# A second norm whose scale moves to the logits and gates, row sums taken from the attention values, one expert choice for all tokens, and a sum of experts on TensorE

## The reference

```python
def _L1_attn_ref(x):
    scores = jnp.einsum('bsd,btd->bst', x, x)
    attn_weights = jax.nn.softmax(scores, axis=-1)
    return jnp.einsum('bst,btd->bsd', attn_weights, x)

def _L1_ffn_ref(x, router_w, router_b, expert_w, expert_b):     # E = 8, K = 2
    router_probs = jax.nn.softmax(x @ router_w + router_b, axis=-1)
    top_p, top_i = jax.lax.top_k(router_probs, K)
    top_p = top_p / jnp.sum(top_p, axis=-1, keepdims=True)
    expert_out = jnp.einsum('bnd,edc->bnec', x, expert_w) + expert_b
    gathered = jnp.take_along_axis(expert_out, top_i[..., None], axis=2)
    return jnp.einsum('bnk,bnkc->bnc', top_p, gathered)

x = x + _L0_conv_ref(_gn(x), ...)
t = _to_tokens(x)
t = t + _L1_attn_ref(_ln_t(t))
t = t + _L1_ffn_ref(_ln_t(t), ...)
```

## Time and profile before

| | us |
|---|---|
| median of 3 executions | 107.4 (107.09 to 108.33) |
| profiled execution, its own time | 108.61 |
| its span | 106.9 |
| TensorE matmul busy (533 instructions) | 78.2 (73%) |
| VectorE busy (127) | 67.1 (63%) |
| GpSimd busy (73) | 44.1 (41%) |
| ScalarE busy (66) | 30.8 (29%) |
| mean granted TensorE clock | 0.837 |

### The profile page before, as it was taken

How to read it: one execution, slowest core, us unless ns; L and a number is a source line. 1 busy time by engine, 2 the same in 40 slices (tenths; PEclk the granted TensorE clock), 3 DMA queues, 4 the chain that set the end, 5 groups by cost and what they waited for, 6 DMA issues and landing times.

```text
span 106.9 us, 1448 instructions
## 1 busy us (share of the span) xinstructions
PE 78.2 (73%) x533; PEld 65.0 (61%) x533; DVE 67.1 (63%) x127; ACT 30.8 (29%) x66; POOL 44.1 (41%) x73
## 2 busy tenths in 40 slices
PE   3797999489801995599399965979448899957820
PEld 3696499389602994599399954956124588933400
DVE  2046200427968999907828934882997268989990
ACT  0441000696991410100740002154934130101100
POOL 6019999700526999999300000000003300494440
PEclk9999999999985599859999999999975555695555
DMA  0214300028400000000000000000000000000022
GB/s 26 83 32 92 62 8 0 6 65 257 123 0 3 0 0 0 0 0 6 3 0 0 0 0 3 6 0 0 0 0 0 0 6 0 0 0 0 3 46 53
DMA packets 5115, 2.36 MB, mean 22 GB/s; under 512 B 4290, under 2 KB 4643, under 8 KB 5107
## 3 DMA queue, kind: packets, MB, share of 16 engines
q1 hardware_dynamic: 4675, 2.06, 8.1%
q10 hardware_dynamic: 432, 0.20, 0.7%
HBM read 0.81 MB, written 0.26 MB: 10 GB/s over the span
## 4 chain that ended last, share of the span: by engine, by line
PE 40%; DVE 35%; ACT 11%; issue 6%; DMA 3%; DVEq 1%; POOL 1%; POOLq 0%
DVE image_all L936 8%; PE ps L580 7%; PE ps L492 7%; PE ps L532 5%; DVE prod L288 4%; DVE att_d L1084 4%; DMA x_rows<-in_x 3%; ACT absoff L777 2%; DVE image_all L1132 2%; PE ps L592 2%; ACT hat L781 2%; PE ps L692 2%; PE ps L522 2%; PE ps L654 2%; DVE prod L1167 2%
## 5 line engine op out<-in xcount | busy, mean ns | idle before, releaser
L580 PE MATMUL ps<-wide_ident,prod 128*128 128x128 f32 x81 | 13.0, 334 | 9.5 <-DVE prod L288 9.5
L580 PEld LDWEIGHTS ps<-wide_ident,prod 128*128 128x128 f32 x81 | 12.2, 178 | 10.3 <-DVE prod L288 5.6
L936 DVE TENSOR_TENSOR image_all<-ps,images 128x1024 f32<-128x1024 f32 (+3 forms) x8 | 14.2, 1818 | 6.4 <-PE ps L580 6.4
L492 PE MATMUL ps<-wide_ident 128*128 128x128 f32 x70 | 14.4, 367 | 1.8 <-POOL wide_ident L367 1.8
L492 PEld LDWEIGHTS ps<-wide_ident 128*128 128x128 f32 x70 | 12.8, 270 | 4.0 <-issue 2.2
L476 POOL TENSOR_TENSOR prod<-prod,tok 128x256 f32<-128x256 f32 x2 | 1.9, 964 | 30.3 <-DVE prod L1091 30.3
L592 PE MATMUL ps<-wide_ident,image_all 128*128 128x128 f32 x100 | 12.0, 274 | 0.0
L592 PEld LDWEIGHTS ps<-wide_ident,image_all 128*128 128x128 f32 x100 | 11.0, 141 | 0.2 <-DVE image_all L936 0.2
L483 POOL TENSOR_TENSOR image_all<-image_all 128x512 f32<-128x512 f32 (+1 forms) x6 | 6.0, 1008 | 11.1 <-DVE image_all L1132 10.9
L284 POOL TENSOR_TENSOR my<-prob,hat 128x384 f32<-128x384 f32 x8 | 7.8, 1000 | 2.3 <-DVE ps L284 2.3
L288 DVE TENSOR_TENSOR prod<-ps,hat 128x1152 f32<-128x1152 f32 x6 | 7.9, 1351 | 0.4 <-ACT ps L797 0.3
(11 more groups left out here) (171 smaller groups left out, 131.4 us busy)
## 6 DMA issues: line engine op xcount, KB each, us to landing
images<-images SPq DMA_DIRECT2D x2, 300.0 KB, 4.1
images<-images SPq DMA_DIRECT2D x2, 280.0 KB, 3.5
x_tok<-in_x SPq DMA_DIRECT2D x4, 64.0 KB, 2.3
out_dram<-prod SPq DMA_DIRECT2D x3, 64.0 KB, 2.2
x_rows<-in_x SPq DMA_DIRECT2D x1, 128.0 KB, 2.7
x_rows<-in_x ACTq DMA_DIRECT2D x1, 128.0 KB, 3.1
expert<-in_expert_w SPq DMA_DIRECT2D x4, 32.0 KB
out_dram<-prod ACTq DMA_DIRECT2D x1, 64.0 KB, 2.5
```

What stands on the lines that cost most here:

```text
L492: pe.matmul(pbank(bank, P), ident, ident, start=True, stop=True)
L580: ins = pe.matmul(coef_rows(ty, tx, tx + 1), prod[:, ky, dy, kx * D + dx, :], ident, start=first[tx // 4], stop=((ky, dy) == PAIRS_OF_ROW[ ...
L936: v.tensor_tensor(taps[:, ty % SLOTS, t0:t1, :, :], bcast(coef_rows(ty, t0, t1).rearrange("p (t j) -> p t j", j=P), 2, GC), images[:, t0:t ...
```

## The change

- Attention: TensorE multiplies the exponentials by `tok_q` = `tok_ln` + 1 in place of `tok_ln` (made on POOL). As the 32 normed channels sum to zero, the 32 values of a token sum to 32 times its row sum. So VectorE reduces the 128x256 values of a group once (`attended`) in place of the eight reductions of 128x512, and 1 is subtracted again when the values are added to `tok_c` and, through `tok` - 1 (also on POOL), to the residual.
- Second norm: `channels_first` turns `tok_c` without its scale. The logits are multiplied by the reciprocal deviation afterwards (`logits(ga)`), and so are the gates of the experts (`gate_s`); the gates of the expert biases stay unscaled (`gate`, on POOL). The router bias is added on VectorE.
- First norm: the two groups are interleaved step by step, and `scores(0)` comes before `channels_first` of group 1.
- One `choose()` over both groups, with tiles of 128x128 and 128x16.
- TensorE sums the experts: `sum_experts` multiplies the identity by the gated values of one expert at a time, eight products for two images (128 columns) or one image (64 columns), five such blocks, into the bank that holds the residual. POOL's L483 and L484, VectorE's L1167 and `finish` go. ScalarE copies the result out.
- `keep_warm` goes in three places of the tail, has 11 in place of 12 products in the first norm, and has 18 products between `experts(4)` and `turn_gates()`.

The diff, cut to its core:

```diff
-WARM = {..., "token norm": 12, "lnT": 2, "second norm": 3, "second norm, last group": 6, "ln2T": 2}
+WARM = {..., "token norm": 11, "choice": 18}
...
-        EXPERT = (7, 0, 5, 6)
+        LOGITS = (1, 0)
+        EXPERT = (7, 5, 6, 1, 0, 7, 5, 6)
...
+            for ga in range(GA):
+                g.wait_ge(tok_normed, ga + 1)
+                g.tensor_scalar(tok_q[:, t, :], tok_ln[:, t, :], 1.0, None, ALU.add).then_inc(values_ready, 1)
+                g.tensor_scalar(tok[:, t, :], tok[:, t, :], -1.0, None, ALU.add).then_inc(values_ready, 1)
...
-            for pair in range(GA * GI // 2 - 1):
-                g.wait_ge(gated_ready, 2 * pair + 2)
-                for n in (NE * C // 2, NE * C // 4):
-                    then(g.tensor_tensor(x[:, :, 0:n], x[:, :, 0:n], x[:, :, n:2 * n], ALU.add))
-                g.tensor_tensor(moe[...], x[:, :, 0:C], x[:, :, C:2 * C], ALU.add).then_inc(pair_summed, 1)
+            g.wait_ge(rtotal_ready, 1)
+            g.wait_ge(chosen, 1)
+            g.tensor_tensor(gate[:, :, :], second[:, :, :], bcast(top[:, 4, :], 2, NE), ALU.mult).then_inc(gate_ready, 1)
...
+            def sum_experts(ga, q0, q1):
+                pe.wait_ge(gated_ready, ga * GI + q1)
+                total = pbank(PV + ga, GT * C).rearrange("p (h q c) -> p h q c", h=HALVES, q=GI)[:, :, q0:q1, :]
+                for e in range(NE):
+                    ins = pe.matmul(total, ident, gated[:, ga, q0:q1, :, e, :].rearrange("p q h c -> p h q c"),
+                                    start=False, stop=(e == NE - 1 and q1 == GI), skip_group_check=True)
+            def experts(n):
+                ga, q = n // GI, n % GI
+                if n >= 5:
+                    pe.wait_ge(gated_ready, n - 4)
+                elif n >= 3:
+                    pe.wait_ge(logits_kept, n - 2)
+                for h in range(HALVES):
+                    ins = pe.matmul(...)
...
             for ga in range(GA):
                 pe.wait_ge(tok_normed, ga + 1)
                 channels_first(2 - ga, tok_ln, ga).then_inc(lnT_done, 1)
+                scores(ga)
+            weighted(0)
+            att_to_tokens(0)
+            weighted(1)
+            pe.wait_ge(tok2_centred, 1)
+            channels_first(2, tok_c, 0).then_inc(ln2T_done, 1)
+            att_to_tokens(1)
+            pe.wait_ge(late_ready, 4)
+            router(0)
+            pe.wait_ge(tok2_centred, 2)
+            channels_first(2, tok_c, 1).then_inc(ln2T_done, 1)
+            router(1)
+            for n in range(3):
+                experts(n)
+            residual(0)
+            residual(1)
+            experts(3)
+            experts(4)
+            keep_warm(2, WARM["choice"])
+            turn_gates()
+            experts(5)
+            chosen_bias(0)
+            chosen_bias(1)
+            experts(6)
+            experts(7)
+            sum_experts(0, 0, 2)
+            sum_experts(0, 2, 4)
+            sum_experts(1, 0, 2)
+            sum_experts(1, 2, 3)
+            sum_experts(1, 3, 4)
...
             def attended(ga):
+                then(v.tensor_reduce(att_d[:, g], o, AX, ALU.add))
+                then(v.reciprocal(att_r[:, g], att_d[:, g]))
+                v.scalar_tensor_tensor(out=att[:, g, :], in0=o, scalar=float(C), in1=bcast(att_r[:, g], 2, C),
+                                       op0=ALU.mult, op1=ALU.mult).then_inc(att_ready, 1)
...
+            v.tensor_copy(attT[:, 0, :], pbank(PV, HALVES * P)).then_inc(attT_ready, 1)
+            attended(0)
+            sum_squares(0, tok2_squared).then_inc(tok2_summed, 1)
+            attended(1)
+            v.wait_ge(late_ready, 4)
+            logits(0)
+            sum_squares(1, tok2_squared).then_inc(tok2_summed, 1)
+            logits(1)
+            choose()
             gated_experts(0)
             gated_experts(1)
```

More of the change, by code:

```diff
@@ L61 @@
 WARM = {"start": 3, "group sums": 3, "squares": 2, "normalised": 1, "layer norm": 0,
-        "projection weights": 1, "token norm": 12, "lnT": 2, "second norm": 3,
-        "second norm, last group": 6, "ln2T": 2}
+        "projection weights": 1, "token norm": 11, "choice": 18}
 def bcast(ap, dim, n):
@@ L196, in hybrid_block @@
         ln2T = late_part(2).rearrange("p (a h t) -> p a h t", a=GA, h=HALVES)
+        logit = sb("logit", [P, NT, NE])
         lsame = sb("lsame", [P, NT, NE])
@@ L687, in experts @@
[L687 to L694, removed]
+                pe.wait_ge(att_ready, ga + 1)
@@ new lines, in experts @@
+            def experts(n):
[4 more added lines that the diff above has]
+                    pe.wait_ge(logits_kept, n - 2)
+                for h in range(HALVES):
+                    ins = pe.matmul(pbank(EXPERT[n], NE * C, h * NE * C), ln2T[q * C:(q + 1) * C, ga, h, :],
+                                    expert4[q * C:(q + 1) * C, :, :], start=True, stop=True)
+                ins.then_inc(experts_done, 1)
@@ L1061, in by_deviation, with tokens @@
                 scale(ga, dst, normed)
-            v.wait_ge(x_tok_ready, 1)
-            for ga in range(GA):
+            def tokens(ga):
                 v.wait_ge(conv_out, ga + 1)
@@ L1122, in choose @@
[L1122 to L1126 removed]
+                v.reciprocal(rtotal, total).then_inc(rtotal_ready, 1)
@@ new lines, in choose @@
+                then(v.tensor_tensor(second[:, :, :], marks, bcast(mark, 2, NE), ALU.is_equal))
+                v.wait_ge(rtotal_ready, 1)
+                v.tensor_tensor(scaled, rtotal, tok_r[:, :], ALU.mult)
+                then(v.tensor_tensor(second[:, :, :], second[:, :, :], bcast(e, 2, NE), ALU.mult))
+                v.tensor_tensor(second[:, :, :], first[:, :, :], second[:, :, :], ALU.add).then_inc(chosen, 1)
+                v.wait_ge(chosen, 1)
+                then(v.tensor_tensor(gate_s[:, :, :], second[:, :, :], bcast(scaled, 2, NE), ALU.mult))
@@ L1133, in gated_experts @@
                                     bcast(by_image[:, q, :, :], 3, C), ALU.mult).then_inc(gated_ready, 1)
-            for n in range(GI - 1):
-                row_sums(n)
-            then(row_sums(GI - 1))
-            then(v.reciprocal(att_r[:, group(0)], att_d[:, group(0)]))
-            row_sums(GI)
-            row_sums(GI + 1)
             v.wait_ge(pv_done, 1)
             v.tensor_copy(attT[:, 0, :], pbank(PV, HALVES * P)).then_inc(attT_ready, 1)
-            row_sums(GI + 2)
             attended(0)
-            then(row_sums(GI + 3))
```

223 lines of the change are left out of this document (96 added, 127 removed).

## The result

The changed kernel takes 113.45 us (median of 4 executions, 112.32 to 114.17), the kernel before 107.87 (107.09 to 110.94): a ratio of 1.051, 95% interval 1.035 to 1.066. It is slower, as forecast, by 5.6 us on the medians where 4.1 was forecast. The executions of one kernel differ by some microseconds, and the ratios leave out the slowest ones.

The account below looks back on a forecast made before the run. VectorE alone bounds the old kernel's last ten microseconds; TensorE would bound the changed one. Gates turned at 95.0 plus 13.1 end at 108.1 against 103.98, losing 4.1: 107.4 becomes 111.5 us, range 109.8 to 112.8, widened to 108.5 to 113.8.

Parts of the forecast that it names:

- the forecast's own range: Whole kernel: 109.8 to 112.8 us around the forecast 111.5, given chance 0.63.
- the wider one: Whole kernel: 108.5 to 113.8 us, widened for an early clock rise and most of a second fall.
- a second fall of the clock: Clock falls again after the gates are turned; sum starts at 0.50, +1.7 to +3, 113.2 to 114.5 us; chance 0.09.
- Up to the router: First norm to second norm: `router(1)` starts at 82.3 where it started at 92.99, worth 10.7 us.
- The clock: TensorE at 0.50 from between 79 and 84, back 3.8 us after `keep_warm` starts, at 93.0; gates turned at 95.0.
- TensorE after the turning: Turning, experts, bias, the sum's 80 instructions at 0.112 and ScalarE's copy at clock 1.00: together 13.1 us.
- the forecast 108.1: End of the tail: the result is there at 108.1, against 103.98 in the kernel before.
- the rival of a cheap sum: TensorE's sum at 0.056 for each instruction, 2.2 to 4.5 us less, 109.3 to 107.0 us; chance 0.08.
- VectorE and GpSimd: Choice from 83.9 takes 4.7 us, gates at 88.6; POOL's 128x256 additions some 0.4 each without cover.
- That the clock never falls: Clock never falls or is back before `experts`; result at 102.9, kernel at 106.3 us; chance 0.08.
- That VectorE would be the bound: End of the kernel: gating ends at 93.6 and VectorE sets the end, 99.5 us; chance 0.02.

Follow-up runs that it names:

- run 1: Changed kernel without its 18 `keep_warm` products before the gates are turned: 111.63 us, ratio 1.034 to the kernel before.
- run 4: Changed kernel with TensorE's sum in two blocks of 256 columns, 32 instructions in place of 80: 110.9 us, ratio 1.032 to the kernel before.
- run 2: Changed kernel with ten identity products put into TensorE's waits and 11 in place of 18 before the turning: 107.83 us, ratio 0.989 to the kernel before.
- runs 3: Changed kernel with the expert sum back on GpSimd and VectorE and without the 18 products: 104.88 us, ratio 0.964 to the kernel before.
- 5 (held clock): Changed kernel with ten inserted products, 11 before turning, experts 5 to 7 in one run, GpSimd summing group 0, TensorE group 1: 103.56 us, ratio 0.960.
- 6 (two choices): Changed kernel with ten inserted products, whole sum on GpSimd and VectorE, experts chosen once for each group, gates turned after experts 5 to 7: 104.49 us, ratio 0.967.
- 6 (one choice): Changed kernel with inserted products (10 and 11), experts 5 to 7 in one run, whole sum on GpSimd and VectorE, single choice: 103.33 us, ratio 0.964.
- run 7: Changed kernel with inserted products (10 and 11), experts 5 to 7 in one run, TensorE's sum in two blocks of 256 columns: 105.76 us, ratio 0.968.
- run 8: Shared-sum kernel with inserted products, sum in three parts: GpSimd group 0, TensorE group 1's first pair, VectorE its second: 101.85 us, ratio 0.941 to the kernel before.

## Why the prediction was right

The mechanism came out step by step, and the size less well: the median, 113.45, is 0.65 above the forecast's own range (109.8 to 112.8) and inside the wider one only in the part that was added for a second fall of the clock, which the trace of the changed kernel does not show. That the wider range holds is in part luck.

**Up to the router: right.** 10.7 us were forecast for `router(1)`, at 82.3. The changed kernel has it at 83.89, but its mark lies 0.9 later and its output products took longer (below); run 1 and run 4, whose output products ran at full clock, have it at 82.24 and 81.36, that is 16.2 us behind the mark, as the forecast 82.3 is (82.3 - 66.1). The exponential followed the scores by 1.16, as worked out. One reading in the prediction is off without effect: by the earlier trace rows the clock of the kernel before fell at 78.79 and not at 78.9.

**The clock: right in its place, by a hair generous in its size.** It fell between 79 and 84 (83.75) and was back 3.1 us after the start of `keep_warm`, where I had put 3.8. Gates turned at 95.0 were forecast, 96.49 measured in a trace whose tail is late by the 1.6 us told of below. Two of the three rises from which the 3.8 was read, at 37.84 and 48.07, came behind unbroken transpositions of 128x128 (L580) and not behind products as the prediction says. Run 2, with run 1 beside it, turned the cause from argued into shown.

**TensorE after the turning: right to 0.1 us.** 13.1 from the turning to the end of ScalarE's copy, against 13.1 (96.49 to 109.55): bias 1.06 for 0.95, the others as forecast, the sum 9.15 for 9.3. The 0.112 for each instruction of 128 or 64 columns held (9.15 us for 80, 0.114 each), and run 4 shows it by itself (0.224 with 256 columns). So the rival of a cheap sum, at 0.056 for an instruction, is out.

**VectorE and GpSimd.** Choice from 85.50 to the gates at 90.29 is 4.8, forecast 4.7 (14 instructions of 0.32 and three of 0.2 would add up to 5.1; the small ones overlap their neighbours in part: one of 0.17 started at 89.26, and the next instruction at 89.35). GpSimd's additions of 1 took 0.85 each and not 0.4, a miss that cost nothing, since the values were needed only at 76.84.

**What was sized too small: the whole.** The forecast was 4.1 us, and 5.6 lie between the medians. The profiled execution shows where its own difference comes from. The mark is 0.9 later, and the output products, before anything of the change, took 2.55:

```profile
66.98 2.55 PE L628 MATMUL ps<-w_out_bd,sampT 128*64 128x64 f32 x32 [0.78 <-DVE sampT L1068]
```

against 1.5 in the kernel before (66.12 to 67.63), because the clock had fallen at 66.69 here. The same fall, between 66.0 and 66.8, stands in the traces of runs 3, 5 (held clock) and 6 (two choices), so it comes and goes with the execution and not with the edit. The later mark and these products made the router of group 1 late by 1.6 us against the forecast, and the end of the tail came 1.45 after the forecast 108.1: in this trace it is the whole miss. Whether it is also the 1.5 us between forecast and medians was not separated, and stays open: four executions of the changed kernel are few for a spread of 2 us, and only one of them has a trace, so a second fall of the clock in the others is not excluded.

**The rivals.** That the clock never falls is out by the trace; run 2 shows that it can be made true up to the turning, and that the kernel is then 1.1% faster than before. That this is the rival's number is a coincidence: run 2 turned its gates 1.1 us earlier against the mark than the rival had it, with 11 products in place of 18, and lost 1.2 again where the clock fell under the sum (10.38 in place of 9.15). That it falls again behind the turning didn't happen in the profiled execution, but did in those of runs 2, 5 (held), 6 (one choice), 7 and 8, which all hold the clock up to the turning; 0.09 was too low a chance for such work in these kernels. That VectorE would be the bound needed TensorE free, as foreseen.

## What to carry to other kernels

Before work is moved to an engine that looks idle, price it by instructions at the clock which that engine will have there: here 80 instructions, 0.114 us each at clock 1.00 also where they had only 64 columns, took over 9 us at the end of the kernel, while three engines sharing the sum, with the clock held, make the whole kernel some 10% faster than that. A light stretch of TensorE was paid for here in the stretch behind it (busy 1.92 of 3.75 us up to 83.75 in the changed kernel, then clock 0.50 until 93.99, under router and experts); a few products put into waits that are there anyway (ten here, no delay, and 7 fewer before the turning) brought 5 us, where products put in front of the work (18 here, 5.7 us) brought nothing. What a held clock is worth depends on who carries the end: 5 us with the whole sum on TensorE, 1 to 2.5 with half of it there, nothing to 1.5 with the sum on GpSimd and VectorE.

## What the runs showed of the hardware

- Products that use different 32 rows of the array shared their time when they were issued together: `experts` of one image, two images or three images took the same 1.1 us at clock 1.00 (1.13 for one in the changed kernel; run 7: 1.14 for two, 1.15 for three) and 2.1 at 0.50 (run 1: 2.07, 2.08 and 2.10), and four took 2.04 to the start of the next product at 0.50 in the kernel before. Where the three had to wait for gatings 0.62 apart (run 7), they took 2.32.
- VectorE's reduction of 128x1024 took 1.93 us beside GpSimd's additions in run 8, as before the change (1.88), and the instructions of 128x64 took up to 1.19 for 0.23 beside them (run 6, two choices); the gating, which reads one operand from PSUM, kept its 0.62 beside the same additions (eight in 4.88 in run 6, one choice, with GpSimd's first pair from 88.91 on).
